# Layer 1 attention of a hybrid kernel: the softmax sums taken over six key tiles per ones-product instead of four, on one core

## The reference, cut to what matters

```
dots = einsum('bhid,bhjd->bhij', q, k) * scale
attn = softmax(dots, axis=-1)
out = einsum('bhij,bhjd->bhid', attn, v)
```

## Time and profile before

| | us |
|---|---|
| median of three runs | 7087.46 |
| the profiled execution, timed from outside | 7073.67 |
| its span, first to last instruction | 7071.9 |
| TensorE busy in the span | 6629.5 (94%) |
| VectorE | 5324.9 (75%) |
| GpSimd | 4330.6 (61%) |
| ScalarE | 4099.1 (58%) |
| attention of layer 1, first product for the maxima to last sum | about 1584 to 5953 |

### The profile page before, as it was taken

One profiled execution on the slowest core, in us unless ns is written; L12 is line 12 of the kernel. 1 busy time (PEld: TensorE's weight loads), 2 busy tenths in 40 slices (PEclk: granted clock), 3 DMA queues, 4 the chain that ended last, 5 costly groups with the idle time before them and its releaser, 6 DMA issues. The chain is left out here.

```text
span 7071.9 us, 127529 instructions
## 1 busy us (share of the span) xinstructions
PE 6629.5 (94%) x44776; PEld 4171.2 (59%) x44776; DVE 5324.9 (75%) x12960; ACT 4099.1 (58%) x9510; POOL 4330.6 (61%) x3066
## 2 busy tenths in 40 slices
PE   8599998989999999999999999999999998749999
PEld 5477776655554554555554555555555554648898
DVE  5499896658877876887886787787787882549998
ACT  2399994224666666666666666666666665424444
POOL 5111112334887887887887787787787785355564
PEclk9799999998999999999999999999999999879999
DMA  8633425774446446446446446546546335652221
GB/s 250 135 75 84 84 61 155 251 235 96 86 96 139 87 97 138 88 89 141 93 86 134 101 86 137 102 88 132 104 86 136 75 77 119 167 115 62 67 61 33
DMA packets 481792, 786.11 MB, mean 111 GB/s; under 512 B 74784, under 2 KB 352530, under 8 KB 477175
## 3 DMA queue, kind: packets, MB, share of 16 engines
q0 software_dynamic: 119408, 349.08, 24.8%
q1 hardware_dynamic: 361735, 428.76, 23.7%
HBM read 300.82 MB, written 188.46 MB: 69 GB/s over the span
## 5 line engine op out<-in xcount | busy, mean ns | idle before, releaser
L1436 DVE TENSOR_REDUCE a_tops<-a_ps 128x1 f32<-128x448 f32 x5600 | 3085.2, 613 | 960.0 <-PE a_ps L1332 938.9
L1542 ACT ACTIVATE a_P<-a_ps 128x448 f32<-128x448 f32 (+1 forms) x5600 | 2657.9, 547 | 1599.1 <-PE a_ps L1406 1494.7
L1406 PE MATMUL a_ps<-a_qp,a_kp 98*128 98x448 f32 (+1 forms) x5600 | 2185.3, 395 | 32.2 <-ACT a_P L1542 27.4
L1559 POOL TENSOR_TENSOR a_later<-a_P 128x896 f32<-128x896 f32 x672 | 1514.1, 2253 | 412.9 <-ACT a_P L1542 412.9
L1406 PEld LDWEIGHTS a_ps<-a_qp,a_kp 98*128 98x128 f32 (+1 forms) x5600 | 1036.4, 186 | 1216.6 <-ACT a_P L1542 801.3
L1332 PE MATMUL a_ps<-a_kp,a_qp 96*128 96x448 f32 x4704 | 1751.7, 382 | 2.0 <-DVE a_tops L1436 0.6
L1559 POOL TENSOR_TENSOR a_four<-a_P 128x896 f32<-128x896 f32 x672 | 1440.1, 2224 | 332.7 <-ACT a_P L1542 332.1
L1358 PE MATMUL a_ps<-a_P,a_vt 128*32 128x448 f32 (+1 forms) x11200 | 1338.5, 549 | 0.0
L1332 PEld LDWEIGHTS a_ps<-a_kp,a_qp 96*128 96x128 f32 x4704 | 879.3, 187 | 223.1 <-DVE a_tops L1436 157.3
L1572 POOL DMA_DIRECT2D a_four<-a_later x672 | 584.8, 870 | 215.4 <-POOL a_later L1559 133.3
L682 ACT ACTIVATE n_P<-n_sm,n_mx 112x280 f32<-112x280 f32 x896 | 468.0, 522 | 96.9 <-DVE n_mx L629 96.7
(11 more groups left out here) (201 smaller groups left out, 8466.9 us busy)
## 6 DMA issues: line engine op xcount, KB each, us to landing
a_four<-a_later POOLq DMA_DIRECT2D x672, 448.0 KB, 4.2
a_qp<-scratch_q SPq DMA_DIRECT2D x168, 224.0 KB, 6.0
a_hk<-scratch_k SPq DMA_DIRECT2D x84, 392.0 KB, 7.9
a_kp<-scratch_k SPq DMA_DIRECT2D x96, 320.0 KB, 6.4
scratch_t<-o_ts SPq DMA_DIRECT2D x56, 448.0 KB, 5.8
n_vt<-scratch_vw SPq DMA_DIRECT2D x64, 343.0 KB
e_w<-in_w SPq DMA_DIRECT2D x16, 1024.0 KB
scratch_vw<-p_vs SPq DMA_DIRECT2D x56, 224.0 KB
```

The costliest lines, as they stand in the source:

```text
L1406: pe.matmul(PS[0:rows_of(t), i_s % 3, 0:GW], kp[0:98, hh, 128 * t:128 * t + rows_of(t)], qp[0:98, hh, GW * j:GW * j + GW], start=True, sto ...
L1436: dve.tensor_reduce(tops[0:rows_of(t), slot, k:k + 1], PS[0:rows_of(t), bank, 0:GW], AX_X, ALU.max).then_inc(topped, 1)
L1542: act.activation(P[0:rows_of(t), (2 * n + pair) % (2 * RING), hh % 2, :], PS[0:rows_of(t), (4 * n + hh) % 3, 0:GW], ACT.Exp).then_inc(expe ...
L1559: pool.tensor_tensor(out, P[:, (2 * n + pair) % (2 * RING), :, :], P[:, (2 * n + 2 + pair) % (2 * RING), :, :], ALU.add).then_inc(added, 1)
```

## The change

A sum is now taken over six tiles. `PAIRS // 3` = 4 sixes replace the 6 fours. GpSimd adds the first pair of tiles of a six into `six` and the second pair into `later[:, 0]`, and issues one accumulating DMA of 896 KB for all four heads; then it adds the third pair into `later[:, 1]`, waits for the first DMA to land, and issues a second accumulating DMA onto the same destination. The odd tile is added by GpSimd to the third part of the last six (two more adds, 64 partitions); its ones-product is gone. The ones-product of a six stands six steps behind its last tile. `yo` is gone: the division writes into `y`, one step later than before, and `take` waits for the store of `y`. The ring `P` stays at five tiles.

```diff
@@ sizes and buffers
-        FOURS = PAIRS // 2
-        SUMS = FOURS + 1
+        SIXES = PAIRS // 3
+        SUMS = SIXES
+        ADDS = 2 * PAIRS + 2
-        SUM_LAG = 5
+        SUM_LAG = 6
-        four = sb("four", [128, 4, 2, GW])
-        later = sb("later", [128, 3, 2, GW])
+        six = sb("six", [128, 2, 4, GW])
+        later = sb("later", [128, 2, 4, GW])
-        yo = sb("yo", [128, GW])
@@ bursts()
-                if t % 4 == 3:
-                    sums.append((n, (n // STEPS, j, t // 4)))
+                if t % 6 == 5 and t < KT - 2 or t == KT - 1:
+                    sums.append((n, (n // STEPS, j, (t - 1) // 6)))
@@ TensorE: mix and the ones-product
-                if t == KT - 1:
-                    for hh in range(4):
-                        last = pe.matmul(PS[HD * hh:HD * hh + HD, SUM, 0:GW], ones[0:rows, :],
-                                         P[0:rows, (2 * n + hh // 2) % (2 * RING), hh % 2, :], start=False,
-                                         stop=SUM_NUMBER[j, FOURS] == LAST_SUM[j])
-                    last.then_inc(summed, 1)
-
-            def sum_four(q, j, f):
-
-                for pair in range(2):
-                    pe.wait_ge(joined[f % 2][pair], 16 * (q * (FOURS * NG // 2) + (FOURS * j + f) // 2 + 1))
+
+            def sum_six(q, j, f):
+
+                pe.wait_ge(joined[f % 2][1], 16 * (q * (SIXES * NG // 2) + (SIXES * j + f) // 2 + 1))
...
@@ VectorE
-                w = (j - 1) % NG % 2
-                since(dve, stored[w], q, 16 * ((NG + 1 - w) // 2), 16 * ((j + 1) // 2))
-                dve.tensor_tensor(yo[:, :], y[:, :], sums[:, :], ALU.mult).then_inc(divided, 1)
+                dve.tensor_tensor(y[:, :], y[:, :], sums[:, :], ALU.mult).then_inc(divided, 1)
-                        if 6 <= n % KT < 10:
+                        if 7 <= n % KT < 11:
-                        if n % KT == 10:
+                        if n % KT == 11:
@@ ScalarE
             def take(q, j):
-                since(act, divided, q, NG, j)
+                w = (j - 1) % NG % 2
+                since(act, stored[w], q, 16 * ((NG + 1 - w) // 2), 16 * ((j + 1) // 2))
...
-                                if t0 == KT - 1:
-                                    act.wait_ge(summed, (q + before) * (SUMS * NG) + SUM_NUMBER[j0, FOURS])
-                            if t0 < KT - 1:
-                                act.wait_ge(added, (q + before) * (2 * PAIRS * NG) + 2 * (PAIRS * j0 + t0 // 2) + pair + 1)
+                            act.wait_ge(added, (q + before) * (ADDS * NG) + ADDS * j0 + 2 * (t0 // 2) + pair + 1)
@@ GpSimd
-            def join(q, j, f, pair):
-
-                number = FOURS * j + f
-                kept_in = later[:, (2 * number + pair) % 3, :, :]
-                if pair == 1:
-                    at = q * (FOURS * NG) + number - 1
-                    if not isinstance(at, int) or at >= 0:
-                        pool.wait_ge(joined[(f - 1) % 2][0], 16 * (at // 2 + 1))
-                add(q, j, 2 * f + 1, pair, kept_in)
-                pool.wait_ge(added, q * (2 * PAIRS * NG) + 2 * (PAIRS * j + 2 * f + 1) + pair + 1)
-                pool.dma_start(four[:, 2 * (f % 2) + pair, :, :].rearrange("p a n -> p (a n)"),
-                               kept_in.rearrange("p a n -> p (a n)"), accum_op=ALU.add).then_inc(joined[f % 2][pair], 16)
+            def add_last(q, j, pair):
+
+                out, n = later[0:KTAIL, 1, 2 * pair:2 * pair + 2, :], KT * j + KT - 1
+                pool.wait_ge(exped, q * HS + 4 * n + 2 * pair + 2)
+                pool.wait_ge(added, q * (ADDS * NG) + ADDS * j + 2 * (PAIRS - 1) + pair + 1)
+                pool.tensor_tensor(out, out, P[0:KTAIL, (2 * n + pair) % (2 * RING), :, :], ALU.add).then_inc(added, 1)
+
+            def join(q, j, f, part):
+
+                number = q * (SIXES * NG) + SIXES * j + f
+                last = f == SIXES - 1 and part == 1
+                pool.wait_ge(added, q * (ADDS * NG) + ADDS * j + (ADDS if last else 6 * f + 2 * part + 4))
+                if part == 1:
+                    pool.wait_ge(joined[f % 2][0], 16 * (number // 2 + 1))
+                pool.dma_start(six[:, f % 2, :, :].rearrange("p a n -> p (a n)"),
+                               later[:, part, :, :].rearrange("p a n -> p (a n)"), accum_op=ALU.add)\
+                    .then_inc(joined[f % 2][part], 16)
...
-                        for pair in range(2):
-                            add(q, j, 2 * f, pair, four[:, 2 * (f % 2) + pair, :, :])
-                        for pair in range(2):
-                            join(q, j, f, pair)
+                        for pair in range(2):
+                            add(q, j, 3 * f, pair, six[:, f % 2, 2 * pair:2 * pair + 2, :])
+                        for part in range(2):
+                            if number >= 1:
+                                pool.wait_ge(joined[(f - 1) % 2][part], 16 * ((number - 1) // 2 + 1))
+                            for pair in range(2):
+                                add(q, j, 3 * f + 1 + part, pair, later[:, part, 2 * pair:2 * pair + 2, :])
+                            if f == SIXES - 1 and part == 1:
+                                for pair in range(2):
+                                    add_last(q, j, pair)
+                            join(q, j, f, part)
```

More of the change, by code:

```diff
@@ L1053, in layer1_attend @@
         scored, exped, added, mixed, summed = sem("scored"), sem("exped"), sem("added"), sem("mixed"), sem("summed")
-        joined = [[sem("joined%d%d" % (w, pair)) for pair in range(2)] for w in range(2)]
+        joined = [[sem("joined%d%d" % (w, part)) for part in range(2)] for w in range(2)]
         taken, sums_taken = sem("taken"), sem("sums_taken")
@@ L1150, in layer1_attend @@
                     order.append(part[1:])
-                elif part[2] % KT == KT - 1:
-                    order.append((part[1], part[2] // KT, FOURS))
         own = [(j, u) for quad, j, u in order if quad == 0]
@@ L1163, in layer1_attend @@
         TAKE_AT = [burst_of(lambda p: p[:3] == ("mix", 0, KT * j + KT - 1)) + 1 for j in range(NG)]
-        TAKE_SUMS_AT = [burst_of(lambda p: p[0] == "sum" and p[1:3] == (0, j) or p[:3] == ("mix", 0, KT * j + KT - 1)) + 1
+        TAKE_SUMS_AT = [burst_of(lambda p: p[0] == "sum" and p[1:3] == (0, j)) + 1
                         for j in range(NG)]
@@ L1245, in quad @@
                             sp.sem_inc(steps, 1)
-                            sp.dma_start(S["y1T"][q - 1, :, GW * (NG - 1):N], yo[:, :])\
+                            sp.dma_start(S["y1T"][q - 1, :, GW * (NG - 1):N], y[:, :])\
                               .then_inc(stored[(NG - 1) % 2], 16)
@@ L1269, in quad @@
                         sp.sem_inc(steps, 1)
-                        sp.dma_start(S["y1T"][q, :, GW * (n // KT - 1):GW * (n // KT)], yo[:, :])\
+                        sp.dma_start(S["y1T"][q, :, GW * (n // KT - 1):GW * (n // KT)], y[:, :])\
                           .then_inc(stored[(n // KT - 1) % 2], 16)
@@ L1295, in _ @@
             sp.sem_inc(steps, 1)
-            sp.dma_start(S["y1T"][QUADS - 1, :, GW * (NG - 1):N], yo[:, :])\
+            sp.dma_start(S["y1T"][QUADS - 1, :, GW * (NG - 1):N], y[:, :])\
               .then_inc(stored[(NG - 1) % 2], 16)
@@ L1374, in sum_four @@
                 for hh in range(4):
-                    last = pe.matmul(PS[HD * hh:HD * hh + HD, SUM, 0:GW], ones[:, :],
-                                     four[:, 2 * (f % 2) + hh // 2, hh % 2, :],
+                    last = pe.matmul(PS[HD * hh:HD * hh + HD, SUM, 0:GW], ones[:, :], six[:, f % 2, hh, :],
                                      start=(f == 0), stop=SUM_NUMBER[j, f] == LAST_SUM[j])
@@ L1384, in burst @@
                     else:
-                        sum_four(q + part[1], part[2], part[3])
+                        sum_six(q + part[1], part[2], part[3])
             def quad(q, first, more):
@@ L1485, in quad @@
                     if j >= 0 or not first:
-                        if 6 <= n % KT < 10:
-                            invert(q if j >= 0 else q - 1, j % NG, n % KT - 6)
-                        if n % KT == 10:
+                        if 7 <= n % KT < 11:
+                            invert(q if j >= 0 else q - 1, j % NG, n % KT - 7)
+                        if n % KT == 11:
                             divide(q if j >= 0 else q - 1, j % NG)
@@ L1575, in quad @@
             def quad(q):
                 for j in range(NG):
-                    for f in range(FOURS):
-                        before, at = divmod(FOURS * j + f - 2, FOURS * NG)
-                        since(pool, summed, q + before, SUMS * NG, SUM_NUMBER[at // FOURS, at % FOURS])
+                    for f in range(SIXES):
+                        number = q * (SIXES * NG) + SIXES * j + f
+                        before, at = divmod(SIXES * j + f - 2, SIXES * NG)
+                        since(pool, summed, q + before, SUMS * NG, SUM_NUMBER[at // SIXES, at % SIXES])
```

## The result

The changed kernel takes 7048.08 us in the median (7022.55 to 7056.21), the kernel before 7087.46: a ratio of 0.9945, interval 0.9935 to 0.9955, or 39 us less. The direction was forecast, the size was not: 99 us and a range of 6960 to 7078 around 6988. The measured time is in the range, but the gain is 0.4 of the forecast one. The profiled execution took 7042.71 us, 31 less than that of before.

What follows compares the result with a forecast made beforehand. TensorE was taken to set the pace, busy 543.8 of 550 us mid-attention. The terms -126 + 18 + 4 + 5 = -99 us, taken from the median 7087.46, gave 6988 us, range 6960 to 7078.

Steps and rivals of the forecast that it cites:

- What bounds the kernel, and the ones-products: TensorE sets the pace in the attention; 168 fewer ones-product bursts of 0.75 us each save 126 us.
- GpSimd's work and the issue: GpSimd's own adds and DMA issues per group: 64.2 us after, 64.8 before, hidden under TensorE's 71.3; issue 0.87 us.
- The transfer: Accumulating DMA of twice the bytes: 2.4 us more transfer, so 6.6 us from issue to landing.
- In the last six the odd tile's adds lie inside that wait: Last six of a group: GpSimd's odd-tile adds fit into its wait for the first DMA; cost in quiet stretches nothing.
- Where loads collide: Last group of each quad, DMA engines full: +18 us, 2.3 per quad; bounds nothing and the whole excess, 90 in all.
- the lag of the sum: Second DMA lands 13.2 us after the first's issue, the ones-product burst comes about 18 us after it: cost nothing.
- Dividing one step later ... Nothing: Division one step later, into y itself, and storing from y lie beside this work: no cost.
- Loads needed many steps later. Nothing: The store holds SP's queue 2.7 us longer, but the loads behind it are needed many steps later: no cost.
- Light steps and the tail: Steps after the last maxima, where GpSimd's chain exceeds TensorE's six: +4 us; wait for the last DMA: +5 us.
- The chain as the bound: Rival: GpSimd's loop with a slow first DMA (8.5 us) outlasts TensorE's six, giving 7148 us, slower; chance 0.13.
- VectorE as the pace of the dense groups: Rival: VectorE paces the dense groups, so 16 of 56 groups gain nothing, giving 7024 us; chance 0.05.
- contention costs all of its bound: Rival: colliding loads at the quads' ends cost the full 90 us, giving 7060 us; chance 0.10.

Runs made afterwards that it cites:

- Lag 7: The changed kernel with the ones-product one step later, which also moves the division to step 12: 6986.71 us, ratio 0.9850 to the kernel before.
- without the loads: Keys, values and heads for the maxima loaded for the first quad only: ratio 0.9928 for the kernel before, 0.9827 for the changed kernel.

## Why the prediction was right and wrong

- *What bounds the kernel, and the ones-products: right.* 168 bursts of 0.75 us; the quiet groups went from 74.7 to 72.4 us.
- *GpSimd's work and the issue: right.* The issue took 869 ns in the median (872 before), and the ring held: ScalarE waited 37 us for GpSimd's adds where it waited 97. In the timeline of a quiet stretch the chain stalls GpSimd for a microsecond, as forecast, and it catches up:

```profile
2989.32 4.55 POOL L1545 TENSOR_TENSOR a_later<-a_P 128x896 f32<-128x896 f32 x2 [0.32 <-ACT a_P L1528]
2994.90 0.87 POOL L1562 DMA_DIRECT2D a_six<-a_later  x1 [1.04 <-DMA a_six<-a_later]
2995.64 4.33 POOL L1545 TENSOR_TENSOR a_six<-a_P 128x896 f32<-128x896 f32 x2
```

- *The transfer: right,* 6.4 us for 6.6. By the fit in the Trainium skill (DMA: Bandwidth & Descriptors, Anatomy of one DMA) the added bytes cost 1.05 us on top of the 4.2 measured, so 5.3, an estimate; the measurement decides, and with it the rival of the cheap transfer is out.
- *"In the last six the odd tile's adds lie inside that wait": wrong.* By the prediction's own figures 0.60 + 4.5 us of adds and the odd tile's 4.2 come to 9.3 us, more than the 6.6 of the landing. In the trace the second DMA of a group's last six went out 9.6 us behind the first in the median, in the other sixes 6.9 to 7.2.
- *Where loads collide, and with it the lag of the sum: the step that failed, in size.* The term was 2.3 us per quad, 18 in all, and the cost of the lag was "nothing again". The steps lost 82 of the 126 us. The budget of 18 us for both landings was worked out and then tried on 6.6 + 6.6 only. TensorE waited 49 us for landings ahead of the last one, in two ways. In group 1 one landing of 15 to 17 us was enough, as shown above. In group 6 both landings were slow, 7 to 10.6 us each. In that group of the third quad the first DMA went out at 3228.58, the second at 3239.47, and TensorE's burst began at 3249.26, behind an idle time of 5.65 us:

```profile
3228.58 0.87 POOL L1562 DMA_DIRECT2D a_six<-a_later  x1 [0.30 <-POOL a_later L1545]
...
3239.47 0.86 POOL L1562 DMA_DIRECT2D a_six<-a_later  x1 [5.83 <-ACT a_P L1528]
```
```profile
3249.26 1.72 PE L1366 MATMUL a_ps<-a_six,a_ones 128*32 128x448 f32 x8 [5.65 <-DMA a_six<-a_later]
```

  That is 20.7 us from the first issue, with landings of 10.4 and 9.8 us: where both are slow by some four microseconds, the burst is late by twice that. Lag 7 took 40 to 56 us off. The bound of "the whole excess" was also built on bytes, and what was lost was latency. The DMA share of the 80 us hardly rose, 0.87 for 0.86; taken from the first to the last step of group 6, it went from 0.82 to 0.86 before to 0.83 to 0.95 after in the seven quads with loads. Why one landing takes 16 us beside the heads' loads is not shown.
- *The half clock was no term at all.* It grew from 20.5 to 146.8 us inside the steps. The kernel before had it too, in five short pieces, and a row of it stood among those read: the last ones-product took 1.72 us behind its wait, where it takes 0.96.
- *"Dividing one step later ... Nothing": wrong.* The move put the division where GpSimd adds. Moving it one step on gave 28 us with the loads and 25 without (good to 13 and 19 us), and in both traces the long steps 12 are gone. It was priced by its place in the order, not by what runs on GpSimd at that time.
- *"Loads needed many steps later. Nothing": wrong for one load.* The fourth value load is issued at step 173 and its part awaited at the first mix of the next quad. The held queue is not the reason, since the store stands eleven steps ahead of it in SP's list. In the two quads where TensorE waited, the load landed after 16.1 and 16.9 us, in the others after 7 to 11. Counting it to the second part gave 16 us at lag 6.
- *Light steps and the tail: right in the sum, 9.7 us for 9, not in the parts.* The last quad's group 6 took 68.9 us for 63.9 with three bursts fewer, so 7 us were lost in it, for the 4 of the term; 2.6 of them are a wait for a landing. The last wait is 10.00 us for 5.82, and from the last score to the next stage it was 2.4 us more, for the 5 of the term.
- *The rivals.* The chain as the bound is refuted: the quiet groups kept their 71.9 to 73.3 us in every run with four bursts, while GpSimd waited up to 209 us, but for the few that a division held and the last quad's group 5 (69.3). VectorE as the pace of the dense groups is refuted too: without the loads group 0 gained 17 of its 18 us. The result lies at 7048, next to the case that "contention costs all of its bound" (7060, chance 0.10), but by the sum of three mechanisms of which that case held one, so by luck.

Open: how the 147 us at half clock split between the waits themselves and work that ran slower was not measured alone. Open too is the kernel before with a later sum.

## What to carry to other kernels

When two waits are chained, try the budget on the slowest landings of the trace and not on the median, once with both slow and once with only the last; count too what else holds the second issue. A consumer one step later cost nothing here, since the buffers allowed it. When an instruction of VectorE with two inputs in SBUF is moved, look at what GpSimd does at the new place. And when a stage gets faster, list each load by the steps between its issue and its wait: the shortest one is the next bound.

## What was not expected of the hardware

A division of 448 elements per partition took 0.61 to 4.91 us by when it was issued beside GpSimd's adds. TensorE fell to 1.2 GHz around waits of 2.2 and 4.0 us, and the step after the longer one took 5.31 us for 3.22. An accumulating DMA of 896 KB took 6.2 us to land at best, 6.4 in the median and 16.9 at worst, beside the heads' loads. One packet of 7,168 bytes of it took 554 ns in the median, one of 3,584 bytes 291 ns: nearly in proportion.
